# Constant matmuls in TensorE's waits, and the first attention's head choice as four masked output weights, in a four-layer network on one core

## The chip, the core and the metric

The kernel runs on one core of a Trainium2 chip. A core has engines that each work through an instruction list of their own in order: TensorE (PE; its weight loads are shown apart as PEld), VectorE (DVE), ScalarE (ACT), GpSimd (POOL) and SyncE (SP), the last issuing most DMAs. They meet through semaphores: an instruction raises one, another engine waits until it has reached a number. PSUM has eight banks of 128 x 512 float32 into which TensorE writes and from which DVE and ACT read. The metric is device time of the whole program in microseconds (us), less is better.

## The reference, cut to what matters

The input is x of shape (4, 512, 128), 2048 tokens of 128 features. Four layers follow each other, each an attention-like part and a feed-forward part; each part's result is added to x and the sum goes through a layer norm without weights. The parts differ from layer to layer: attention inside windows of 32 tokens with 16 heads of 8 features, then 16 experts (4 of them per token) and a shared one; attention by directions with 8 heads, then 8 experts of limited capacity; rotary attention with 8 heads of 128, then a block of rotary attention with 16 heads of 64 and 31 experts; a gated linear recurrence with a small feed-forward, then 8 experts. Only the first attention's arithmetic is arranged anew by the change:

```python
qkv = jnp.einsum('bglc,cd->bgld', xg, w_qkv)
q, k, v = jnp.split(qkv, 3, axis=-1)
q = rmsnorm(q, ln_w); k = rmsnorm(k, ln_w)
# 16 heads of 8 features, windows of 32 tokens
att = jnp.einsum('bghqd,bghkd->bghqk', q, k) * scale
att = softmax(where(causal, att, -max))
y = jnp.einsum('bghqk,bghkd->bghqd', att, v)
y = y.transpose(0, 1, 3, 2, 4).reshape(Bx, Tx, Cx)
return jnp.einsum('btc,cd->btd', y, w_proj)
```

## The kernel before, in words

x lies in SBUF feature-major, 128 features on the partitions and 2048 tokens along the rows, worked on in B = 4 blocks (chunks) of T = 512 columns. The program is a row of stages, in this order, with the names that the profile shows: load; window attention (`l0a`); norm with the router's logits, router and experts of layer 0 (`f_n0a`, `r`, `e`); norm and scores, then the direction attention (`a1p`, `a1`); norm, capacity router, capacity experts (indirect DMAs carry tokens to the experts' slots in DRAM and back); norm and rotary attention with whole heads (`a2f_n1f`, `a`); norm and rotary attention with two heads per unit (`h`), router, experts; norm and recurrence (`rc`); norm, router with a hidden layer, experts; a last norm with the store (`n3f`). Between stages `recycle` (L115) clears the semaphores and puts a barrier over all engines. Most stages begin with a `Head` (L259): TensorE centres each block (`centre`, L218 to 221: a matmul of the sum with `center_w`), ACT squares, TensorE takes the mean of squares (`variance`, L237 to 241), ACT makes the inverse root, DVE scales. A wait on `PEq L119` in the trace is this barrier's.

Inside a stage the order of every engine is written out by hand, as a list of calls with the semaphore waits between them. Nothing plans or reorders it; what an engine does next is what stands next in its list. So TensorE idles where its next instruction's inputs are not there.

Window attention (L405 to 664) takes one chunk at a time: chunk 0, a loop over chunks 1 and 2, then chunk 3. Per chunk TensorE does the scores (`scores`, L492 to 504, 64 small products of 32 rows), the previous chunk's output product (`out`, L509 to 511), the next chunk's projections (`front`, L478 to 490), and the values (`values`, L513 to 526). Each group of 32 partitions in the four PSUM banks of the values holds four heads side by side although a partition's feature belongs to only one of them. DVE picks the right head: with masks in `vecs` columns 1 to 4 it forms `y_fm` as a sum of four masked slices (L642, three times L644), and `out` multiplies that with `wproj`.

A float32 matmul of the program appears in the trace as two records: the centre product of one block is `x2`.

The routers (L1017) compute logits, wait for DVE to find the best experts, and then transpose the gates on TensorE (L1096). Experts (L718) run `hidden` (L855 to 857: products of rounded parts) ahead of `output` (L871 to 874). In the capacity experts (L1387) POOL issues 32 indirect DMAs (L1417), SP waits for all of them and loads the slots (L1429), TensorE turns them (L1444).

## Time and profile before

| | |
|---|---|
| median of 3 runs | 1823.33 us (1818.88 to 1825.23) |
| the profiled execution, its own time | 1824.96 us |
| its span | 1823.2 us |
| TensorE busy | 1552.0 us (85%) |
| VectorE busy | 1033.2 us (57%) |
| ScalarE busy | 1005.3 us (55%) |
| GpSimd busy | 758.9 us (42%) |
| mean granted TensorE clock | 0.918 |

The profiled execution is one run of the program; its span is from the first to the last instruction. Busy time is the time in which an engine executes, summed; TensorE's includes matmuls at whichever clock was granted. The granted clock is 1.0 at 2.4 GHz and 0.5 at 1.2 GHz. In a row of the timeline `[8.74 <-DVE r_g_tm L1187]` says that the engine had been idle for 8.74 us and that the instruction which released it was DVE's, on tile r_g_tm, in line 1187.

### The profile page before, as it was taken

What the parts mean: (1) busy time and instruction counts of PE and PEld (TensorE: products, weight loads), DVE (VectorE), ACT (ScalarE), POOL (GpSimd) and SP (SyncE); (2) the same over time, 40 slices, a digit from 0 to 9 for tenths busy, and PEclk for the clock granted to TensorE, in tenths of its full rate; (3) what the DMA queues carried; (4) which work ended last, traced back from release to release, by engine and by line L of the source; (5) the groups of instructions that cost most, each with busy time, mean ns of one, the idle gap of its engine ahead of it and who ended that gap; (6) DMA issues with size and microseconds to landing.
All of it is one profiled execution on the core that took longest, in us unless ns stands there. A gap on an engine that the chain in (4) does not pass through costs nothing. (4 is left out here: it accounts for less than half of the span.)

```text
span 1823.2 us, 27092 instructions
## 1 busy us (share of the span) xinstructions
PE 1552.0 (85%) x8756; PEld 999.4 (55%) x8756; DVE 1033.2 (57%) x2134; ACT 1005.3 (55%) x2164; POOL 758.9 (42%) x704
## 2 busy tenths in 40 slices
PE   5668987860977799999789999999889999858898
PEld 3336743330974566666445555555458886324685
DVE  5955776631214555555356556556458886662675
ACT  4324564550423455555556666656538887664786
POOL 1224530017342566666165655655324442021363
PEclk8968978975888999999999999999979999979899
DMA  1007311021223122222121111111026562000330
GB/s 42 1 15 166 75 61 52 1 96 47 78 65 114 40 60 62 60 59 59 62 55 42 42 48 43 40 47 44 15 89 262 211 217 89 1 0 21 136 113 24
DMA packets 62165, 125.50 MB, mean 69 GB/s; under 512 B 14354, under 2 KB 29571, under 8 KB 55532
## 3 DMA queue, kind: packets, MB, share of 16 engines
q1 hardware_dynamic: 59724, 119.57, 22.5%
q0 software_dynamic: 2304, 4.24, 0.7%
q8 instruction: 69, 1.13, 0.3%
q14 instruction: 68, 0.56, 0.1%
HBM read 79.39 MB, written 11.35 MB: 50 GB/s over the span
## 5 line engine op out<-in xcount | busy, mean ns | idle before, releaser
L1857 ACT ACTIVATE h_probs<-psum,h_nmax 128x512 f32<-128x512 f32 (+3 forms) x256 | 133.3, 526 | 126.0 <-DVE h_nmax L1937 68.2
L1937 DVE TENSOR_REDUCE h_nmax<-psum 128x1 f32<-128x512 f32 (+3 forms) x256 | 116.3, 486 | 101.5 <-PE psum L1747 101.5
L897 ACT ACTIVATE psum<-psum,f_b 128x512 f32<-128x512 f32 x200 | 131.8, 659 | 27.4 <-PE psum L857 27.3
L1672 POOL TENSOR_TENSOR h_swapped<-h_swapped,rope_tables 128x512 f32<-128x512 f32 x64 | 81.8, 1278 | 153.8 <-DMA h_swapped<-h_raw 153.8
L823 POOL TENSOR_TENSOR e_lo<-e_gated,e_hi 128x512 fp32r<-128x512 f32 x59 | 76.1, 1291 | 152.1 <-ACT e_hi L909 152.1
L1857 ACT ACTIVATE a_probs<-psum,a_nmax 128x512 f32<-128x512 f32 (+3 forms) x128 | 67.6, 528 | 125.0 <-DVE a_nmax L1937 76.8
L1672 POOL TENSOR_TENSOR a_swapped<-a_swapped,a2f_a_tables 128x512 f32<-128x512 f32 x64 | 82.8, 1294 | 124.5 <-DMA a_swapped<-a_raw 124.4
L932 DVE TENSOR_TENSOR e_lo<-psum,e_hi 128x512 fp32r<-128x512 f32 x168 | 114.8, 683 | 26.5 <-ACT psum L897 26.5
L855 PE MATMUL psum<-f_x_hi,f_w_hi 128*128 128x512 f32 x272 | 109.2, 402 | 5.9 <-DVE e_gated L946 4.1
L1744 PE MATMUL psum<-h_k,h_q 64*128 64x384 f32 (+3 forms) x512 | 104.9, 486 | 7.5 <-POOL h_k L1677 5.0
L1754 PE MATMUL psum<-ident,h_probs 128*128 128x128 f32 x640 | 108.7, 277 | 0.6 <-ACT h_probs L1857 0.4
L856 PE MATMUL psum<-f_x_hi,f_w_lo 128*128 128x512 f32 x272 | 108.5, 399 | 0.0
L857 PE MATMUL psum<-f_x_lo,f_w_hi 128*128 128x512 f32 x272 | 108.3, 398 | 0.0
L1937 DVE TENSOR_REDUCE a_nmax<-psum 128x1 f32<-128x512 f32 (+3 forms) x128 | 62.5, 489 | 71.0 <-PE psum L1747 69.8
L1744 PE MATMUL psum<-a_k,a_q 128*128 128x512 f32 (+3 forms) x256 | 91.9, 442 | 6.2 <-DVE a_wvo L1929 6.2
L874 PE MATMUL psum<-e_lo,f_w_hi 128*128 128x512 f32 x236 | 92.7, 393 | 1.9 <-DVE e_lo L932 0.9
L871 PE MATMUL psum<-e_hi,f_w_hi 128*128 128x512 f32 x236 | 92.6, 392 | 0.0
L872 PE MATMUL psum<-e_hi,f_w_lo 128*128 128x512 f32 x236 | 92.4, 391 | 0.0
L1772 PE MATMUL psum<-h_p_t,h_v 128*64 128x256 f32 (+3 forms) x512 | 89.9, 451 | 0.0
L946 DVE TENSOR_TENSOR psum<-psum,e_gate 128x512 f32<-128x512 f32 x96 | 67.2, 700 | 32.9 <-ACT psum L897 28.6
L1754 PEld LDWEIGHTS psum<-ident,h_probs 128*128 128x128 f32 x640 | 71.6, 141 | 24.0 <-ACT h_probs L1857 19.9
L1772 PE MATMUL psum<-a_p_t,a_v 128*128 128x512 f32 (+3 forms) x256 | 82.4, 444 | 0.0
(471 smaller groups left out, 4024.0 us busy)
## 6 DMA issues: line engine op xcount, KB each, us to landing
e_gate<-gates SPq DMA_DIRECT2D x39, 1024.0 KB, 4.7
a_swapped<-a_raw SPq DMA_DIRECT2D x128, 128.0 KB, 2.3
h_swapped<-h_raw SPq DMA_DIRECT2D x256, 64.0 KB, 2.0
e_gate<-gates SPq DMA_DIRECT2D x16, 512.0 KB, 7.2
f_w<-in_l_experts SPq DMA_DIRECT2D x17, 256.0 KB, 5.0
f_w<-in_l_experts SPq DMA_DIRECT2D x32, 128.0 KB, 4.7
slots<-a_empty SPq DMA_DIRECT2D x1, 2600.0 KB, 7.5
e_got<-slots SPq DMA_DIRECT2D x8, 325.0 KB, 5.6
```

The costliest lines, as they stand in the source:

```text
L855: nc.tensor.matmul(to, w_h, ex.x_hi[:, cols(b)], start=True, stop=False, skip_group_check=True)
L856: nc.tensor.matmul(to, w_l, ex.x_hi[:, cols(b)], start=False, stop=False, skip_group_check=True)
L857: nc.tensor.matmul(to, w_h, ex.x_lo[:, cols(b)], start=False, stop=True, skip_group_check=True).then_inc(hid_ready, 1)
L874: nc.tensor.matmul(to, w_h, lo[:, n % PLACES, :], start=False, stop=True, skip_group_check=True).then_inc(out_done, 1)
L897: nc.scalar.activation(to, hidden_bank(n), ex.act_func, **bias(n)).then_inc(act_ready, 1)
L932: nc.vector.tensor_tensor(lo[:, n % PLACES, :], whole, hi[:, n % PLACES, :].bitcast(F32), ALU.subtract).then_inc(lo_dve, 1)
L1672: nc.gpsimd.tensor_tensor(swapped[:, j, :], swapped[:, j, :], tables[:, 2 * j + 1, :], ALU.mult).then_inc(sin_ready, 1)
L1744: nc.tensor.matmul(ring[j % RING][:, 0:(q + 1) * P], qs[rows, U % 3, q * P:(q + 1) * P], ks[rows, U % 3, 0:(q + 1) * P], start=True, stop= ...
L1754: last = nc.tensor.transpose(ring[j % RING][:, k * P:(k + 1) * P], probs[:, j % 4, k * P:(k + 1) * P], core.ident[:])
L1772: last = nc.tensor.matmul(misc[1][d, k * P:T], stationary, p_t[:, U % 2, h, k, k * P:T], start=k == 0, stop=k == QT - 1, skip_group_check= ...
L1857: nc.scalar.activation(probs[:, j % 4, 0:(q + 1) * P], ring[j % RING][:, 0:(q + 1) * P], ACT.Exp, bias=nmax[:, j % 8:j % 8 + 1], accum_out ...
L1937: nc.vector.tensor_reduce(nmax[:, j % 8:j % 8 + 1], ring[j % RING][:, 0:(q + 1) * P], AX.X, ALU.max, negate=True).then_inc(max_ready, 1)
```

## The change

There is a new helper. It issues `n` float32 matmuls of two tables that stand in SBUF since the load, `mean_w` (128 x 128) and 256 columns of `rope_tables`, into a PSUM bank that nobody reads before it is written again. Its results are used nowhere. It is called at 45 places of TensorE's order (the seven heads of the direction attention's lead count one each), 225 matmuls in all: at the ends of stages (3 each), behind the stages' heads, and ahead of waits for other engines.

```diff
+def keep_busy(core, pe, bank, n):
+
+    for _ in range(n):
+        core.nc.tensor.matmul(core.psum[:, bank, 0:T // 2], core.mean_w[:], core.rope_tables[:, 0, 0:T // 2], start=True, stop=True)
...
     def tensor(self, pe):
         first, second = self.first, self.second
+        if not first.center:
+            keep_busy(self.core, pe, 7, 3)
```

In the window attention the choice of the head moves from DVE into the weights: four copies of `wproj`, each masked to the features of one head of its group, are made once by DVE, and `out` accumulates four products over head slices. The values are copied out of PSUM as they are, by ACT (in the last chunk half by ACT, half by DVE).

```diff
                 def out(c):
-                    pe.wait_ge(y_ready, c + 1)
-                    nc.tensor.matmul(ps_o[0], wproj[:], y_fm[:].rearrange("p w t q -> p t w q"), start=True, stop=True).then_inc(out_ready, 1)
+                    pe.wait_ge(y_ready, W * c + W)
+                    of_head = o_sb[:].rearrange("p w (t h q) -> p h t w q", h=HG, q=L)
+                    for h in range(HG):
+                        last = nc.tensor.matmul(ps_o[0], wproj_of[:, h, :], of_head[:, h, :, :, :], start=h == 0, stop=h == HG - 1)
+                    last.then_inc(out_ready, 1)
...
                     if not last:
                         front(c + 1)
+                    else:
+                        keep_busy(core, pe, 7, 12)
                     values(c, first, last)
+                    if last:
+                        keep_busy(core, pe, 0, 3)
...
-                pe.wait_ge(mask_ready, 1)
+                pe.wait_ge(mask_ready, 1 + HG)
                 front(0)
                 per_chunk(pe, chunk)
                 out(B - 1)
+                keep_busy(core, pe, 0, 2)
...
+                    act.wait_ge(av_ready, c + 1)
+                    if not first:
+                        act.wait_ge(out_ready, c)
+                    for w in range(2 if last else W):
+                        nc.scalar.activation(o_sb[:, w, :], ps_o[w], ACT.Copy).then_inc(y_ready, 1)
...
-                    dve.wait_ge(av_ready, c + 1)
-                    o = core.psum[:, 4:8, :].rearrange("p w (t h q) -> p (w t) h q", h=HG, q=L)
-                    to = y_fm[:].rearrange("p w t q -> p (w t) q")
-                    for h in range(HG):
-                        if h == 0:
-                            step(nc.vector.tensor_scalar(to, o[:, :, h, :], vecs[:, 1:2], None, ALU.mult))
-                        else:
-                            mix = nc.vector.scalar_tensor_tensor(to, o[:, :, h, :], vecs[:, 1 + h:2 + h], to, ALU.mult, ALU.add)
...
+                    if last:
+                        dve.wait_ge(av_ready, c + 1)
+                        dve.wait_ge(out_ready, c)
+                        for w in range(2, W):
+                            nc.vector.tensor_copy(o_sb[:, w, :], ps_o[w]).then_inc(y_ready, 1)
...
+                for h in range(HG):
+                    nc.vector.tensor_scalar(wproj_of[:, h, :], wproj[:], vecs[:, 1 + h:2 + h], None, ALU.mult).then_inc(mask_ready, 1)
```

The other calls of the helper, the important ones in the order of the program:

```diff
@@ experts: before the first hidden, and at the end @@
+                if not ex.gate_output:
+                    keep_busy(core, pe, 0, 4)
...
+                keep_busy(core, pe, 0, 3)
@@ router: before the wait for the gates @@
+                keep_busy(core, pe, 3, 20 if kind == "sigmoid_groups" else 7 if hidden else 0)
                 pe.wait_ge(gates_ready, 1)
@@ capacity router: before its wait @@
+                keep_busy(core, pe, 3, 10)
                 pe.wait_ge(chosen_ready, 1)
@@ capacity experts: 28 of the 32 indirect DMAs raise sent_first, the last four raise sent @@
+                pe.wait_ge(sent_first, 2 * (NT - 2) * 16)
+                keep_busy(core, pe, 0, 14)
                 turn(0)
...
                 output(E - 1, 1)
+                keep_busy(core, pe, 0, 16)
@@ scores of the directions: at the end, 9 behind a wait for the third block from the end @@
+                pe.wait_ge(rest_ready, len(items) - 3)
+                keep_busy(core, pe, 0, 9)
@@ direction attention: 3 first, 2 behind each of seven heads of the lead, 4 and 3 around second(0) @@
                     first_products(f, m_read)
+                    keep_busy(core, pe, 3, 2)
...
+                keep_busy(core, pe, 3, 4)
                 second(0)
+                keep_busy(core, pe, 6, 3)
@@ rotary attentions: 5 behind the head, 10 (whole heads) or 4 before the first scores @@
                 head.tensor(pe)
+                keep_busy(core, pe, 6, 5)
...
+                pe.wait_ge(raw_ready[1], AHEAD)
+                keep_busy(core, pe, 6, 10 if merged else 4)
                 scores(0)
@@ in the first unit, behind slots 3, 4, 5 and 7 @@
+                    if U == 0 and slot in (3, 4, 5, 7):
+                        keep_busy(core, pe, 7, 2)
@@ recurrence @@
                 z_gate(0)
+                keep_busy(core, pe, 4, 7)
...
                 gates(3)
+                keep_busy(core, pe, 2, 18)
                 out(0)
```

How this stands in the engines' lists. First TensorE at the end of the window attention, chunk 3 and the first products of the norm behind it; before:

```order
L504 MATMUL psum<-l0a_kx,l0a_qn 32x128 x64
L511 MATMUL psum<-l0a_y_fm,l0a_wproj 128x512
L526 MATMUL psum<-l0a_p_t,l0a_v_tm 32x128 x64
L511 MATMUL psum<-l0a_y_fm,l0a_wproj 128x512
L454 UNCONDITIONAL_BRANCH
L1065 UNCONDITIONAL_BRANCH
L221 MATMUL psum<-sum_fm,center_w 128x512 x2
```

and now:

```order
L513 MATMUL psum<-l0a_kx,l0a_qn 32x128 x64
L522 MATMUL psum<-l0a_o_sb,l0a_wproj_of 128x512 x4
L126 MATMUL psum<-rope_tables,mean_w 128x256 x12
L538 MATMUL psum<-l0a_p_t,l0a_v_tm 32x128 x64
L126 MATMUL psum<-rope_tables,mean_w 128x256 x3
L522 MATMUL psum<-l0a_o_sb,l0a_wproj_of 128x512 x4
L126 MATMUL psum<-rope_tables,mean_w 128x256 x2
L463 UNCONDITIONAL_BRANCH
L1085 UNCONDITIONAL_BRANCH
L227 MATMUL psum<-sum_fm,center_w 128x512 x2
```

The names: `l0a_kx`, `l0a_qn` are keys and queries of the scores, `l0a_p_t` the probabilities, `l0a_v_tm` the values, `l0a_o_sb` the copied values. Each output product became four, twelve constant matmuls stand ahead of the last values, three behind them and two at the end.

DVE at the end of a middle chunk and the beginning of the next one's softmax; before:

```order
L70 REGISTER_ALU
L601 TENSOR_SCALAR l0a_kx<-l0a_kn,l0a_vecs 128x16x32 x4
L642 TENSOR_SCALAR l0a_y_fm<-psum,l0a_vecs 128x512
L70 REGISTER_ALU
L644 SCALAR_TENSOR_TENSOR l0a_y_fm<-psum,l0a_vecs,l0a_y_fm 128x512
L70 REGISTER_ALU
L644 SCALAR_TENSOR_TENSOR l0a_y_fm<-psum,l0a_vecs,l0a_y_fm 128x512
L70 REGISTER_ALU
L644 SCALAR_TENSOR_TENSOR l0a_y_fm<-psum,l0a_vecs,l0a_y_fm 128x512
L450 REGISTER_ALU
L450 COMPARE_AND_BRANCH
L620 TENSOR_REDUCE l0a_smax<-psum 128x16
```

and now:

```order
L70 REGISTER_ALU
L623 TENSOR_SCALAR l0a_kx<-l0a_kn,l0a_vecs 128x16x32 x4
L459 REGISTER_ALU
L459 COMPARE_AND_BRANCH
L642 TENSOR_REDUCE l0a_smax<-psum 128x16
```

The four operations on `l0a_y_fm` are gone, so the first maximum (`l0a_smax`) stands directly behind the keys' masks.

TensorE around the first router's end; before:

```order
L1013 MATMUL psum<-f_rw,x_fm 128x16 x16
L714 MATMUL psum<-x_fm,ident 128x512 x4
L1096 MATMUL psum<-ident,r_g_tm 32x128 x16
L1054 UNCONDITIONAL_BRANCH
L838 UNCONDITIONAL_BRANCH
L855 MATMUL psum<-f_x_hi,f_w_hi 128x512
```

and now:

```order
L1033 MATMUL psum<-f_rw,x_fm 128x16 x16
L731 MATMUL psum<-x_fm,ident 128x512 x4
L126 MATMUL psum<-rope_tables,mean_w 128x256 x20
L1117 MATMUL psum<-ident,r_g_tm 32x128 x16
L1074 UNCONDITIONAL_BRANCH
L855 UNCONDITIONAL_BRANCH
L126 MATMUL psum<-rope_tables,mean_w 128x256 x4
L872 MATMUL psum<-f_x_hi,f_w_hi 128x512
```

Twenty constant matmuls stand between the transposes of x (`x_fm`) and the transposes of the gates (`r_g_tm`), and four ahead of the experts' first product.

## Rows read from the trace of the kernel before

**Rows 1.** The page: the span, and the granted clock in 40 slices, in tenths.

```profile
span 1823.2 us, 27092 instructions
...
PEclk8968978975888999999999999999979999979899
```

**Rows 2.** Windows (us, busy us by engine): sum over the 31 half-clock stretches.

```profile
sum 299.02, PE 169.10 PEld 102.00 DVE 121.07 ACT 79.08 POOL 94.48; mean PE 5.45 PEld 3.29 DVE 3.91 ACT 2.55 POOL 3.05
```

**Rows 3.** Windows: sum over the half-clock stretches at seven norm starts.

```profile
sum 37.56, PE 30.69 PEld 12.00 DVE 3.83 ACT 14.17 POOL 5.14; mean PE 4.38 PEld 1.71 DVE 0.55 ACT 2.02 POOL 0.73
```

**Rows 4.** Timeline (start, duration, engine, line): two norm starts.

```profile
108.64 3.75 PE L221 MATMUL psum<-sum_fm,center_w 128*128 128x512 f32 x4 [1.72 <-PEq L119]
...
113.90 1.32 PE L221 MATMUL psum<-sum_fm,center_w 128*128 128x512 f32 x2
...
555.22 1.95 PE L221 MATMUL psum<-sum_fm,center_w 128*128 128x512 f32 x4 [2.04 <-PEq L119]
...
558.09 1.02 PE L221 MATMUL psum<-sum_fm,center_w 128*128 128x512 f32 x2
...
558.95 1.02 PE L241 MATMUL psum<-a2f_n1f_sq,mean_w 128*128 128x512 f32 x2
```

**Rows 5.** Timeline: a middle chunk of the window attention.

```profile
59.21 3.41 PE L526 MATMUL psum<-l0a_p_t,l0a_v_tm 32*32 32x128 f32 x128 [1.36 <-ACT l0a_lnm L559]
...
64.68 0.74 DVE L642 TENSOR_SCALAR l0a_y_fm<-psum,l0a_vecs 128x512 f32<-128x512 f32 x1
...
64.90 1.89 PE L504 MATMUL psum<-l0a_kx,l0a_qn 32*32 32x128 f32 x128 [1.32 <-DVE l0a_kx L601]
65.45 2.32 DVE L644 SCALAR_TENSOR_TENSOR l0a_y_fm<-psum,l0a_vecs,l0a_y_fm 128x512 f32<-128x512 f32 x3
67.69 0.68 DVE L620 TENSOR_REDUCE l0a_smax<-psum 128x16 f32<-128x512 f32 x1
```

**Rows 6.** Timeline: the last chunk of the window attention.

```profile
96.40 5.24 PE L526 MATMUL psum<-l0a_p_t,l0a_v_tm 32*32 32x128 f32 x128 [7.60 <-DVE l0a_p_t L608]
...
96.91 1.96 DVE L608 STREAM_TRANSPOSE l0a_p_t<-l0a_p_sb 128x512 f32<-128x512 f32 x3
...
104.85 2.07 PE L511 MATMUL psum<-l0a_y_fm,l0a_wproj 128*128 128x512 f32 x2 [3.21 <-DVE l0a_y_fm L644]
```

**Rows 7.** Timeline: TensorE at a router and experts; windows: sum over four half-clock stretches there.

```profile
138.22 3.60 PE L1096 MATMUL psum<-ident,r_g_tm 128*32 128x128 f32 x16 [8.74 <-DVE r_g_tm L1187]
...
149.79 0.79 PE L855 MATMUL psum<-f_x_hi,f_w_hi 128*128 128x512 f32 x1 [4.08 <-DVE e_gated L946]
...
1359.18 0.79 PE L855 MATMUL psum<-f_x_hi,f_w_hi 128*128 128x512 f32 x1
...
sum 37.54, PE 23.02 PEld 15.59 DVE 19.51 ACT 9.05 POOL 3.61; mean PE 5.75 PEld 3.90 DVE 4.88 ACT 2.26 POOL 0.90
```

**Rows 8.** Timeline: first product of the capacity experts, and a window behind it.

```profile
453.08 0.97 POOL L1417 DMA_INDIRECT slots<-f_rows,f_slots  x1 [0.30 <-issue]
...
458.30 1.33 PE L1444 MATMUL psum<-ident,e_got 128*128 128x128 f32 x5 [51.38 <-DMA e_got<-slots]
...
458.30:466.07 7.77, 6.93 (x27) 6.56 (x28) 1.75 (x4) 3.37 (x9) 0.00 (x0) 0.50 0.74 267
```

**Rows 9.** Windows: sum over seven half-clock stretches at the other attentions' starts.

```profile
sum 61.46, PE 44.30 PEld 26.66 DVE 28.67 ACT 14.76 POOL 19.70; mean PE 6.33 PEld 3.81 DVE 4.10 ACT 2.11 POOL 2.81
```

**Rows 10.** Timeline: the third attention's first scores.

```profile
581.54 2.05 PE L1744 MATMUL psum<-a_k,a_q 128*128 128x512 f32 x2 [6.20 <-DVE a_wvo L1929]
```

**Rows 11.** Timeline: two waits of TensorE in the recurrence.

```profile
1562.99 3.75 PE L2609 MATMUL psum<-h_xn,h_w_in 128*128 128x512 f32 x4 [4.35 <-DVE rc_xc L2783]
...
1625.98 4.05 PE L241 MATMUL psum<-rc_g_sq,mean_w 128*128 128x512 f32 x4 [12.58 <-POOL rc_g_sq L235]
```

**Rows 12.** Timeline: the end of the first experts.

```profile
225.78 0.69 DVE L975 COPY sum_fm<-psum 128x512 f32<-128x512 f32 x1 [0.22 <-PE psum L874]
...
227.61 3.41 PE L221 MATMUL psum<-sum_fm,center_w 128*128 128x512 f32 x4 [1.86 <-PEq L119]
```

More of the change, by code:

```diff
@@ L1399, in capacity_experts @@
         hid = st.sb("hid", [P, 2, HT, CAPACITY])
-        (w1_split, sent, turned, x_rounded, x_split, hid_psum, hid_ready, out_psum, out_ready, returned, joined) = (st.sem(n) for n in (
-            "w1_split", "sent", "turned", "x_rounded", "x_split", "hid_psum", "hid_ready", "out_psum", "out_ready", "returned", "joined"))
+        (w1_split, sent_first, sent, turned, x_rounded, x_split, hid_psum, hid_ready, out_psum, out_ready, returned, joined) = (st.sem(n) for n in (
+            "w1_split", "sent_first", "sent", "turned", "x_rounded", "x_split", "hid_psum", "hid_ready", "out_psum", "out_ready", "returned", "joined"))
         got_loaded = [st.sem(f"got{e}_loaded") for e in range(E)]
@@ L1417, in _ @@
                         nc.gpsimd.indirect_dma_start(dram["slots"], bass.IndirectOffsetOnAxis(slots[:, k, t:t + 1], 0), rows[:, t, k, :], None,
-                                                     bounds_check=E * CAPACITY - 1, oob_is_err=False).then_inc(sent, 16)
+                                                     bounds_check=E * CAPACITY - 1, oob_is_err=False).then_inc(sent_first if t < NT - 2 else sent, 16)
                 for e in range(E):
@@ L1426, in _ @@
             def _(sp):
-                sp.wait_ge(sent, 2 * NT * 16)
+                sp.wait_ge(sent_first, 2 * (NT - 2) * 16)
+                sp.wait_ge(sent, 2 * 2 * 16)
                 for e in range(E):
@@ L1494, in _ @@
                     last.then_inc(joined, 1)
+                keep_busy(core, pe, 4, 3)
             @block.scalar
@@ L1835, in _ @@
                     between(NU, slot)
+                keep_busy(core, pe, 0, 3)
             @block.scalar
@@ L2344, in _ @@
                         m_read = top_ready, edge_done(f)
+                keep_busy(core, pe, 2, 3)
                 spread_sums(n_units - 1, m_read)
+                keep_busy(core, pe, 2, 5)
                 out(B - 1, (ln_ready, n_units))
+                keep_busy(core, pe, 2, 3)
             @block.scalar
@@ L2679, in _ @@
                     shrink(b)
+                keep_busy(core, pe, 5, 3)
             @block.scalar
```

10 lines of the change are left out of this document (4 added, 6 removed).

## The prediction

> **What bounds the kernel now.** I read the granted clock first. It falls to about 0.5 at stage starts and stays near 1.0 in the long middles [rows 1]; a view of windows over the 31 stretches at 0.5, that is 1.2 GHz, adds up to 299.0 us, in which TensorE is busy for 169.1 us [rows 2]. Work at 1.2 GHz takes twice its time at 2.4 GHz: four records of the centre product take 3.75 us at the half clock and 1.95 us at the full one [rows 4]. So if every stretch were at full clock, TensorE would do its 169.1 us in 84.6 us: 84.5 us is the most that the clock can give, less wherever DVE, ACT, POOL or a DMA sets the pace. What the clock has in common before each fall is a TensorE that waits: 8.74 us at the first router, 7.60 us before the last values, 51.38 us before the capacity experts [rows 6 to 8]. Then I read, stage by stage, which wait ends last.
>
> The Trainium skill, page "TensorE: Matmul & The Clock Gate", section "Terms", prices throttled time at the whole stretch times (1 - K/N), here 299.0 x 0.5 = 149.5 us by an estimate. The trace disagrees: only 169.1 us of the stretches holds TensorE work [rows 2].
>
> **Price of the constant products.** One float32 product of 512 columns follows the next 0.86 us later at full clock (558.09 to 558.95) [rows 4]; half as many columns is 0.43 us, and 0.86 us at the half clock. 225 of them are 97 us at full clock, 194 at half. They cost nothing while they end before the wait they stand in; else the rest is paid. Bounds on what they bring: all 84.5 us, or nothing (a gain below nothing is excluded only where the wait outlasts them at 0.86 us).
>
> **Window attention.** In a middle chunk the scores end at 64.90 + 1.89 = 66.79, but DVE's first maximum starts at 67.69 since it stands behind the y operations (65.45 + 2.32 = 67.77) [rows 5]. Without them it starts some 0.2 us behind the scores, 0.7 us earlier; at three chunk borders 2.1 us. The four ACT copies can run from the values' end (59.21 + 3.41 = 62.62) and are wanted at the scores' end, 4.2 us later: hidden, if ACT is free. The four output products take 3.4 us instead of 0.9 and delay the next projections, whose banks the softmax frees anyway in about 2 us: I take 0; the bound is +1.5 us a border. Four masks of the weights lie before the first product: no row shows 128 x 128; a 128 x 512 of this operation takes 0.74 us [rows 5], so 0 to 3.0 us; I take 0.2 each, 0.8. Last chunk: twelve products (5.2 us) stand in the 7.60 us wait. At full clock the values end when the last transposed group (96.91 + 1.96 = 98.87) has gone through TensorE, about 99.8, instead of 101.64: -1.8. Before, values to output end is 104.85 + 2.07 - 101.64 = 5.3 us [rows 6]; now two copies of about 0.65 in each of two engines, a semaphore, and 3.4 us: 5.1; -0.2. Sum -2.1 + 0.8 - 1.8 - 0.2 = **-3.3**.
>
> **Norm starts.** Seven norms begin at half clock, with 30.69 us of TensorE work [rows 3], so at most 15.3. From the first centre product to the third it is 5.26 us at half (108.64 to 113.90) against 2.87 at full clock (555.22 to 558.09) [rows 4]: 2.4 us at the two coldest, 1.2 to 1.6 at four others, 0.9 at the last: -11.4. The price is the three products at each of nine stage ends: 1.3 us, beside the copy that ends the stage, 0.69 us, and its semaphore [rows 12]. The barrier waits for TensorE too: about 0.45 us each, **+4.0**. Net **-7.4**.
>
> **Routers and experts.** Four stretches hold 23.02 us of TensorE work [rows 7], at most 11.5. First router: 20 x 0.43 = 8.6 us in a wait of 8.74, then the transposes at half of 3.60: -1.8. First experts: 5.7 us of work at half follow 149.79: -2.8. Last router: 7 products (3.0 us) fill less than half of a similar wait: -1.3 of 3.5. Experts of layer 2: the product at 1359.18 is behind no wait [rows 7], four products there are four times 0.43: +1.7, and that they turn the clock is not to be read from a row where TensorE was busy without a pause; 0. Capacity experts: SP still waits for the last indirect DMA, issued at 453.08; 14 products begin about 450.2 (the last four DMAs are issued 0.97 + 0.30 us apart, and the one before them must land) and take 6.0 us; TensorE's first turn was at 458.30. The 6.93 us behind it go at most to 3.5 [rows 8]: -3.0. Capacity router: -0.3. Sum -1.8 - 2.8 - 1.3 + 1.7 - 3.0 - 0.3 = **-7.5**.
>
> **Attentions.** Seven stretches hold 44.30 us of TensorE work [rows 9], at most 22.2, but 28.67 us of DVE lies beside it. In the direction attention DVE paces the lead, so a fraction: -2.5 us for the lead and the first steps (two products per head, 0.86 us, fit a head of 1.9 us only at full clock). Rotary with whole heads: ten products (4.3 us) in the 6.20 us wait [rows 10]: -3.0. With two heads per unit: -2.5. Sum **-8.0**, bounds 0 and -22.
>
> **Recurrence and router of layer 2.** The waits are 4.35 us (seven products, 3.0 us) and 12.58 us (18 products, 7.7 us, before two output products). Behind them 3.75 and 4.05 us at half clock become about 1.95 and 2.1 [rows 11]: -3.7. The rotary norm's first variance: -1.0. Sum **-4.7**.
>
> **Sum.** -3.3 - 7.4 - 7.5 - 8.0 - 4.7 = -30.9. Each term supposes that the clock stays up through its wait. As many waits keep an unfilled rest of 2 to 5 us, I take 0.87 of it: -27. Against the profiled execution's own 1824.96 us (span 1823.2) that is 1798; the runs' median, 1823.33, is 1.6 lower: **1796 us**. No DMA is added or moved past another: POOL still issues the 32 indirect ones in one run, and SP's wait, now on two semaphores, ends with the same last one.
>
> **Rivals.**
> 1. *The clock holds nearly everywhere.* Then half of all half-clock work on a path set by TensorE comes back. For: the stretches are few and short; filling one wait also spares what follows. Against: DVE and POOL are busy 121 and 94 us in the same stretches [rows 2]. Of 84.5 us, I leave out what is beside DVE in the attentions (10), the unfilled stretches (14) and the paid products (10), some 50 remain; less inevitable waits 45: 1824.96 - 45 - 1.6 = 1778.
> 2. *The clock is hardly held.* The products stand too thin in waits of which only a part is filled. Then only the window attention (-2) and a third of the clock's terms come, and the ends still cost 4: some -10, 1813.
> 3. *Slower: the products run at half clock and outlast their waits.* A product is then 0.86 us. The first router's 20 take 17.2 us against 8.74 [rows 7]: +8.5 us; the lead's 14 add 12.0; the capacity experts' 14 take 12.0 against about 8: +4; layer 2's four +3.4; nine ends 2.6 against 0.7: +17. Together 45, of which half is paid if the clock rises midway through each group, as it does before under steady work; less 3 from the window attention: +20, 1843. It decides from the point where groups end later than their wait. Against it: in the cold norm start the clock rises within the work itself, between the first product at 3.75 us for four records and the third at 1.32 for two, where full clock has 1.02 [rows 4].
> 4. *The page's rule.* That a half-clock stretch is paid whole: 1824.96 - 149.5 - 1.6 = 1674 us. As a mechanism of this kernel, other engines' waits would have to shrink with TensorE's clock; in the stretches TensorE is idle for 299.0 - 169.1 = 130 us [rows 2]. It is the rule of the Trainium skill named above.
>
> **How the numbers follow.** Forecast 0.58, rival 1 0.17, rival 2 0.15, rival 3 0.09, rival 4 0.01. The forecast's own range is 1783 to 1809. The range for 8 in 10 goes from 1776 to 1817: it takes in rival 1's middle and most of rival 2, and leaves out rivals 3 and 4 and the tails of 1 and 2. About 0.3% (5.5 us) is what a measurement can tell from no change. Within it lies a third of rival 2 and a little of rival 3 (0.07 in all); slower is most of rival 3: 0.08; faster 0.85.
>
> **What would show it.** Right: the granted clock of the 31 stretches falls from 299 us to under 150; the transposes behind the first router take 1.9 us instead of 3.6; the window attention's last values take about 3.4 us; third minus first centre product is 2.9 us at most norms; the products record 0.43 us each. Wrong: constant products of 0.86 us with the next real product behind them without a wait (rival 3); half-clock sums above 250 us (rival 2); stage ends that cost more than half a microsecond each; or the clock at 1.0 and DVE, ACT or POOL as releasers of every first product, with the same time as before.

## The result, and the profile after

The changed kernel takes 1802.28 us (median of 4 runs, 1797.98 to 1804.23), the kernel before 1824.28 us in the same comparison (median of 4, 1818.88 to 1829.33): a ratio of 0.9873, with a 95% interval of 0.9849 to 0.9896. That is 22 us less, where 27 to 28 were forecast. The profiled execution took 1802.68 us, its span is 1800.9 us.

The page of the changed kernel, the lines that answer to [rows 1], and TensorE's busy time, which was 1552.0 us before:

```profile
span 1800.9 us, 28045 instructions
...
PE 1621.8 (90%) x9230; PEld 1065.9 (59%) x9230; DVE 1018.5 (57%) x2124; ACT 1011.3 (56%) x2178; POOL 756.8 (42%) x704
...
PEclk8999999985998999999999999999979999989999
```

TensorE is busy 70 us longer and the program is 22 us shorter. The granted clock shows why. The windows over the 14 stretches that are left at half clock (us, then busy us by engine, the granted clock in the column before the last two), three of them and their sum, against [rows 2]:

```profile
394.43:442.21 47.78, 4.48 (x11) 3.05 (x11) 8.87 (x25) 0.00 (x0) 31.63 (x32) 0.50 0.13 42
...
568.50:578.75 10.25, 8.81 (x23) 5.68 (x24) 2.88 (x7) 2.65 (x7) 1.74 (x3) 0.50 0.17 38
...
1339.92:1346.74 6.82, 6.82 (x16) 4.78 (x15) 0.19 (x1) 0.66 (x1) 0.00 (x0) 0.50 0.72 236
...
sum 136.70, PE 83.02 PEld 52.48 DVE 49.51 ACT 30.52 POOL 58.15; mean PE 5.93 PEld 3.75 DVE 3.54 ACT 2.18 POOL 4.15
```

31 stretches with 299.0 us became 14 with 136.7 us; the TensorE work in them went from 169.1 to 83.0 us. Of these 83.0 us 11.4 are constant products (the same windows for L126 alone), so the program's own work at half clock fell from 169.1 to about 72 us. Half of that difference, some 48 us, is the most that the clock gave; 22 arrived.

Cut at the first centre product of each norm, the spans of the two traces compare as follows (us, from starts like those in [rows 4]; "again" is a second trace of each, see the experiments):

| stretch that ends at the next norm's start | before | again | after | again | difference of the first two |
|---|---|---|---|---|---|
| load, window attention | 108.64 | 108.45 | 104.32 | 104.44 | -4.3 |
| norm, first router, experts | 118.97 | 118.45 | 114.13 | 114.06 | -4.8 |
| norm, directions | 156.27 | 156.22 | 156.37 | 157.04 | +0.1 |
| norm, capacity router and experts | 171.35 | 168.78 | 167.21 | 164.50 | -4.1 |
| norm, rotary attention | 333.32 | 332.45 | 329.04 | 331.01 | -4.3 |
| norm, two-heads attention, router, 31 experts | 650.92 | 652.11 | 653.49 | 654.55 | +2.6 |
| norm, recurrence | 125.23 | 124.15 | 121.08 | 120.91 | -4.2 |
| norm, last router, experts | 141.93 | 141.27 | 140.21 | 140.24 | -1.7 |
| last norm, store | 16.54 | 16.26 | 15.00 | 15.00 | -1.5 |

**Norms.** The timeline of TensorE at the recurrence's norm, the stage end's products first (start, duration, engine, line):

```profile
1521.38 1.46 PE L126 MATMUL psum<-rope_tables,mean_w 128*128 128x256 f32 x6
1524.57 1.96 PE L227 MATMUL psum<-sum_fm,center_w 128*128 128x512 f32 x4 [1.73 <-PEq L119]
...
1527.43 1.02 PE L227 MATMUL psum<-sum_fm,center_w 128*128 128x512 f32 x2
```

The third centre product now starts 2.86 us behind the first; before it was 5.24 to 5.26 us at the three coldest norms [rows 4]. Over the eight norms this distance adds up to 35.9 us before and 24.8 us after: -11.0. A second trace of the kernel before has 32.3 us, since two more of its norms, the last two, start at full clock unaided (2.87 us); a second trace of the changed kernel has 24.8 again. One norm stays at 4.75 us in the changed kernel, the one before the directions. Its clock is 1.00 too, but a product that waits for a DMA stands ahead of the third centre product:

```profile
222.14 1.13 PE L2511 MATMUL psum<-a1w_spread,a1w_w 24*128 24x256 f32 x4 [0.66 <-DMA a1w_scale<-in_l_scale]
```

**Stage ends.** The end of the first experts, as [rows 12]:

```profile
215.86 1.46 PE L126 MATMUL psum<-rope_tables,mean_w 128*128 128x256 f32 x6
216.06 0.69 DVE L995 COPY sum_fm<-psum 128x512 f32<-128x512 f32 x1 [0.21 <-PE psum L891]
...
218.45 1.95 PE L227 MATMUL psum<-sum_fm,center_w 128*128 128x512 f32 x4 [1.13 <-PEq L119]
```

Six records are three products. From the end of the last real product (215.53 + 0.50 = 216.03) to the norm's first it is 2.42 us, where it was 1.86. At six of the stages' barriers it is +0.56, +0.54, +0.58, +0.55, +0.53 and +0.44: 3.2 us paid. Behind the window attention it is +0.1, at the last experts nothing.

**Window attention**, last chunk, as [rows 6]:

```profile
95.01 2.38 PE L538 MATMUL psum<-l0a_p_t,l0a_v_tm 32*32 32x128 f32 x96 [0.23 <-DVE l0a_p_t L630]
...
97.45 1.08 ACT L602 ACTIVATE l0a_o_sb<-psum 128x512 f32<-128x512 f32 x2 [7.06 <-PE psum L538]
...
98.79 3.70 PE L522 MATMUL psum<-l0a_o_sb,l0a_wproj_of 128*128 128x512 f32 x8
...
102.53 0.69 DVE L634 TENSOR_TENSOR sum_fm<-psum,x_fm 128x512 f32<-128x512 f32 x1 [3.79 <-PE psum L522]
```

The values end at 97.4 at full clock, the copies of ACT and DVE run side by side, and the four output products (eight records) take 3.70 us.

**First router and experts**, as [rows 7]. Eight records are the four products ahead of the experts:

```profile
134.07 1.97 PE L126 MATMUL psum<-rope_tables,mean_w 128*128 128x256 f32 x8 [0.93 <-PEq L1074]
135.69 0.58 PE L872 MATMUL psum<-f_x_hi,f_w_hi 128*128 128x512 f32 x1
...
141.10 0.50 PE L872 MATMUL psum<-f_x_hi,f_w_hi 128*128 128x512 f32 x1 [2.30 <-DVE e_gated L966]
```

The experts' first product is at full clock, and where 4.08 us of wait preceded half-clock work it is now 2.30 us, followed by 3.4 us at half clock.

**Capacity experts**, as [rows 8], with the last indirect DMA:

```profile
442.12 0.97 POOL L1439 DMA_INDIRECT slots<-f_rows,f_slots  x1 [0.30 <-issue]
...
447.38 0.77 PE L1467 MATMUL psum<-ident,e_got 128*128 128x128 f32 x5 [0.34 <-DMA e_got<-slots]
```

From the last indirect DMA's issue to the first turn it is 5.26 us, before 5.22: the turn is as late as its DMA allows. But its five records take 0.77 us instead of 1.33.

**Two places that are paid for.** The two-heads attention's first scores: four products (eight records) stand behind ACT's copy and run at half clock.

```profile
898.00 3.78 PE L126 MATMUL psum<-rope_tables,mean_w 128*128 128x256 f32 x8 [2.78 <-ACT h_raw L1880]
898.89 1.26 POOL L1704 TENSOR_TENSOR h_k<-h_rot,h_swapped 128x512 f32<-128x512 f32 x1
...
901.70 1.76 PE L1771 MATMUL psum<-h_k,h_q 64*128 64x512 f32 x4
```

POOL has `h_k` ready at 898.89 + 1.26 = 900.15, but the scores start at 901.70, behind the products. And the experts of layer 2, where there is no wait at all:

```profile
1336.77 4.06 PE L860 MATMUL psum<-f_gates_t,f_b 32*128 32x512 f32 x8 [0.93 <-PEq L1074]
1340.76 3.78 PE L126 MATMUL psum<-rope_tables,mean_w 128*128 128x256 f32 x8
1343.98 0.99 PE L872 MATMUL psum<-f_x_hi,f_w_hi 128*128 128x512 f32 x1
```

The products take 3.2 us (1340.76 to 1343.98), 0.8 each, inside a stretch at half clock that is there as before, 1339.92 to 1346.74.

**Two places where the wait only moved.** The rotary attention, against [rows 10], and the recurrence, against [rows 11]:

```profile
560.47 4.58 PE L126 MATMUL psum<-rope_tables,mean_w 128*128 128x256 f32 x20 [0.63 <-ACT a_raw L1880]
...
568.98 2.05 PE L1771 MATMUL psum<-a_k,a_q 128*128 128x512 f32 x2 [3.92 <-DVE a_wvo L1962]
```

```profile
1591.25 7.93 PE L126 MATMUL psum<-rope_tables,mean_w 128*128 128x256 f32 x36
1599.02 3.60 PE L2675 MATMUL psum<-rc_h,h_w_out 128*128 128x512 f32 x8
1607.42 4.05 PE L247 MATMUL psum<-rc_g_sq,mean_w 128*128 128x512 f32 x4 [4.80 <-POOL rc_g_sq L241]
```

The first scores of the rotary attention wait 3.92 us behind ten products (twenty records) and stand in a stretch at half clock all the same (568.50). In the recurrence 18 products fill 7.9 us, and 4.80 us of wait for POOL remain: what comes next is set by POOL and DVE.

### The profile page after: what moved, and what is told of

Its sections match the earlier page's. It is cut to its first block and busy times, and to the rows that moved or that the text cites. A ratio compares the mean times of both kernels' runs of the same rounds, so it can differ in the third digit from the quotient of the medians.

```text
span 1800.9 us, 28045 instructions
## 1 busy us (share of the span) xinstructions
PE 1621.8 (90%) x9230; PEld 1065.9 (59%) x9230; DVE 1018.5 (57%) x2124; ACT 1011.3 (56%) x2178; POOL 756.8 (42%) x704
## 5 line engine op out<-in xcount | busy, mean ns | idle before, releaser
L1970 DVE TENSOR_REDUCE h_nmax<-psum 128x1 f32<-128x512 f32 (+3 forms) x256 | 116.1, 485 | 103.9 <-PE psum L1774 103.9
L126 PE MATMUL psum<-rope_tables,mean_w 128*128 128x256 f32 x450 | 111.7, 397 | 50.0 <-DMA slots<-f_rows,f_slots 43.3
L1699 POOL TENSOR_TENSOR h_swapped<-h_swapped,rope_tables 128x512 f32<-128x512 f32 x64 | 81.7, 1276 | 156.3 <-DMA h_swapped<-h_raw 156.3
L126 PEld LDWEIGHTS psum<-rope_tables,mean_w 128*128 128x128 f32 x450 | 86.7, 198 | 70.9 <-DMA slots<-f_rows,f_slots 44.0
```

Source lines behind the costliest of these rows:

```text
L126: core.nc.tensor.matmul(core.psum[:, bank, 0:T // 2], core.mean_w[:], core.rope_tables[:, 0, 0:T // 2], start=True, stop=True)
L1699: nc.gpsimd.tensor_tensor(swapped[:, j, :], swapped[:, j, :], tables[:, 2 * j + 1, :], ALU.mult).then_inc(sin_ready, 1)
L1970: nc.vector.tensor_reduce(nmax[:, j % 8:j % 8 + 1], ring[j % RING][:, 0:(q + 1) * P], AX.X, ALU.max, negate=True).then_inc(max_ready, 1)
```

## The experiments

All were run in groups that share the runs of the kernel before; ratios are to it. A granted clock c over a span s means 2 x (1 - c) x s at half clock. What a trace of an experiment shows inside a stage is given as time from the first centre product of that stage's norm.

**The head choice alone.** The helper issues nothing:

```diff
-    for _ in range(n):
+    for _ in range(0):
```

> The changed kernel with no constant product issued anywhere; the head choice in four masked weights stays. Theory (the two parts are independent, and the head choice is worth what DVE's y operations held on the path): the window attention ends some 2 to 3 us earlier (no clock gain in its last values), everything behind it as before; 1821 us, ratio to before 0.998 to 0.999. Rival (the products carry nothing, the whole gain of 22 us is from the head choice or from where the code lies): 1802. Half-clock time in the 31 stretches: near 299 us by the theory, near 139 by the rival.

1816.46 us (12 runs), ratio 0.9979, interval 0.9954 to 1.0005. Span and mean granted clock:

```profile
core 0: 1814.9 us, clock 0.920
```

0.16 x 1814.9 = 290 us at half clock, as before. The window attention's stretch is 104.2 us against 108.6 and 108.5: -4.3 us, more than expected, and as much as in the changed kernel. The last values end at 97.41 us without any constant product, at 97.39 in the changed kernel, and the norm behind the stage starts at full clock (2.87 us) in both. The gain in the whole is within what the interval allows: it is not told from none.

**The products alone.** The window attention of the kernel before with its own 17 products, all else as changed.

> The 225 constant products as in the changed kernel, the window attention otherwise as before (y formed by DVE, one output product). Theory: 18 to 20 us of the 22 come from the products: 1805, half-clock time near 140 us, norms from first to third centre product 2.9 us. Rival (the four output products in the last chunk are needed to keep the clock for the first norm): the first norm starts at half clock again (third minus first centre product 5.3 us) and 3 us more are lost: 1808.

1801.21 us (6 runs), ratio 0.9893 (0.9868 to 0.9919): all of the gain, as far as can be told. The window attention's stretch is 105.7 us, -2.9 us. So its two halves don't seem to add: each alone brings 3 to 4 us there and both together 4.3, though seven traces of kernels that differ from the changed one at most in the two products at this stage's end have 103.9 to 105.6 us. The first norm's distance is 2.87 us, so the rival, that the norm needs the four output products, is out: the products alone or, in the trace before this one, the output products alone are enough.

**The same places, hardly any work.**

```diff
-        core.nc.tensor.matmul(core.psum[:, bank, 0:T // 2], core.mean_w[:], core.rope_tables[:, 0, 0:T // 2], start=True, stop=True)
+        core.nc.tensor.matmul(core.psum[:, bank, 0:4], core.mean_w[:], core.rope_tables[:, 0, 0:4], start=True, stop=True)
```

> All 225 constant products at their places, but 4 columns wide instead of 256, so that TensorE's order, waits and semaphores are those of the changed kernel and only the work of the products is gone. Theory (what helps is that TensorE is at work in the waits, and so keeps its clock): the half-clock time goes back to 280 to 300 us and the time to about 1819 us (the head choice's 3 to 4 us remain, 4 us for the wider products at stage ends are saved, 4 come from less at the experts of layer 2 and the two-heads attention). Rival (the order, the earlier weight loads or the changed wait on the indirect DMAs bring the gain): 1800, with the half-clock time high all the same. Rival 2 (any activity is enough for the clock): half-clock time stays near 139 us and the time falls below the changed kernel's, about 1792.

1826.93 us (12 runs), ratio 1.0029 (1.0009 to 1.0049): slower than before. The products' line and the clock:

```profile
L126 PE MATMUL psum<-rope_tables,mean_w 128*128 128x4 f32 x450 | 69.9, 282 | 52.6 <-DMA slots<-f_rows,f_slots 43.3 <-PEq L2111 3.0 <-ACT h_raw L1880 2.8
```

```profile
core 0: 1821.5 us, clock 0.921
```

0.158 x 1821.5 = 288 us at half clock. Order, waits and semaphores are those of the changed kernel, so the gain is the clock's and not the order's; both rivals are out. With nothing but their width taken away some 25 to 28 us are lost against the full products (by the medians and by the ratios); against the head choice alone, measured beside it, the kernel is 0.5% slower, about 9 us: the instructions by themselves cost that.

**No products at stage ends.** 26 products gone.

> The changed kernel without the products at the ends of the stages (2 at the window attention's, 3 at the last output of experts, direction attention, rotary attentions, recurrence, capacity experts). Theory of the prediction: each of nine ends costs 0.45 us (in the changed trace about 0.6), and the seven norm starts behind them are at full clock only because of them: the cost of 4 to 5 us goes and 6 to 11 us of norm starts come back, time 1804 to 1808. Rival (the clock would have held over the barrier without them, since what stands before is steady work): norms stay at 2.9 us from first to third centre product and the time falls by 4 to 5 us to about 1797.

1799.55 us (6 runs), ratio 0.9884 (0.9858 to 0.9911), not told apart from the changed kernel. The barriers are back at 1.86 to 2.56 us, so 3.2 us are saved; three of the norm starts fall to half clock again (4.35, 5.25 and 4.23 us from first to third centre product), the directions' is at 5.50 instead of 4.75, and the norm behind the window attention and three more stay at 2.87: 6.0 us lost in the sum over the norms. Both theories were half right: some starts hold their clock over the barrier unaided. The span is 4.7 us shorter in this one trace, mostly in stretches that also differ by 1 to 3 us between two traces of one kernel. Whether the products at stage ends are worth their price is not shown.

**Trim.** No products before the experts of layer 2, none in the first unit of the two-heads attention; there six ahead of the wait instead of four behind it:

```diff
-                if not ex.gate_output:
+                if name == "e0":
                     keep_busy(core, pe, 0, 4)
...
-                    if U == 0 and slot in (3, 4, 5, 7):
+                    if merged and U == 0 and slot in (3, 4, 5, 7):
...
-                pe.wait_ge(raw_ready[1], AHEAD)
-                keep_busy(core, pe, 6, 10 if merged else 4)
+                if merged:
+                    pe.wait_ge(raw_ready[1], AHEAD)
+                keep_busy(core, pe, 6 if merged else 0, 10 if merged else 6)
```

> The changed kernel with three groups taken out or moved: the four products before the experts' first product of layer 2 (the trace of the changed kernel shows no wait there and products at half clock), the eight products in the first unit of the two-heads attention, and its four before the first scores, which become six ahead of the wait instead of four behind it (another PSUM bank). Theory (these three are paid in full: 3.4, 2 to 3, and 1.5 us): the stage from the norm before the two-heads attention to the norm behind its experts, 653.5 us in the changed kernel, falls to 646 to 648, the whole to about 1796. Rival (they hold the clock for what follows, so without them the stretches at half clock grow there): the stage stays at 653 or goes to 656, the whole at 1802 or above.

1798.08 us (5 runs), ratio 0.9844 (0.9820 to 0.9869), whose interval overlaps the changed kernel's. The stretch with the two-heads attention and its experts takes 648.8 us, 4.7 less than in the changed kernel (653.5, again 654.6): 2.9 us of it between the gates' transposes and the experts' first product (7.14 against 10.05 us), 1.9 between the 1st and the 41st record of the scores, 0.5 before them. At the first scores:

```profile
896.32 2.76 PE L126 MATMUL psum<-rope_tables,mean_w 128*128 128x256 f32 x12
...
900.16 1.26 POOL L1704 TENSOR_TENSOR h_k<-h_rot,h_swapped 128x512 f32<-128x512 f32 x1
...
901.47 1.13 PE L1771 MATMUL psum<-h_k,h_q 64*128 64x512 f32 x4 [2.40 <-POOL h_k L1704]
```

Now TensorE waits for `h_k`, as before the change, and not `h_k` for TensorE. Three later kernels with the same trim have 648.0, 647.8 and 650.2 us there. The theory holds; the rival, that these products hold the clock for what follows, does not.

**Doubled at five waits.**

> The changed kernel with the products doubled at five waits, each in a stage of its own: first router 20 to 40, capacity experts 14 to 28, before the rotary attention's first scores 10 to 20, recurrence 18 to 36, last router 7 to 14. Theory (a product costs nothing until its wait ends, then 0.43 us at full clock): first stage with the router +7.7 (8.6 more, 0.9 of wait left), capacity experts +5.5, rotary attention +0.4 (3.9 us of wait left for 4.3) and some of its 10 us at half clock back, -3; recurrence +2.9 (4.8 of wait left for 7.7) less 2.8 for the work at half clock behind it; last router -1 to -2 (3.0 more in 4.4 left). Sum +12: 1814. Rival (half-clock products, 0.86 us each, wherever the wait outlasts the clock): the same sites +17, +12, +4.7, +10, 0; about 1840.

1814.96 us (6 runs), ratio 0.9927 (0.9901 to 0.9953); 1814 was expected. By the ratios it is some 10 us more than the changed kernel, where 12 were expected. The first router:

```profile
121.93 17.43 PE L126 MATMUL psum<-rope_tables,mean_w 128*128 128x256 f32 x80
139.19 1.91 PE L1117 MATMUL psum<-ident,r_g_tm 128*32 128x128 f32 x16
```

Eighty records take 17.43 us, so one product 0.436 us at full clock; the gates' transposes start 35.27 us behind the norm's start, 8.4 us later than without any product (26.91): 40 x 0.436 - 8.76 = 8.7. Sum by stretch against the changed kernel: first router's +9.3, capacity experts' +7.4 (+10.1 against the changed kernel's second trace), recurrence +2.3, last router -0.5, rotary attention -4.6 (in one trace). The rival's 0.86 us per product is out, but for places like the two-heads attention's, where the clock has fallen before the products start.

**None at the same five waits**, 69 products fewer.

> The changed kernel with no products at the same five waits, all others kept. Theory of the prediction: back come 1.8 and 2.8 us in the stage of the first router, 3.0 at the capacity experts, 3.0 at the rotary attention, 1.9 at the recurrence, 1.3 at the last router: +14, 1816; half-clock time from 139 to about 200 us. Rival (the gain sits elsewhere, at the norms and stage ends): +4, 1806.

1806.66 us (6 runs), ratio 0.9889 (0.9864 to 0.9914); the 0.9873 of the changed kernel is not told from it, but the 1816 expected (0.9955) lies above its interval, so +14 us is out. At half clock are 0.092 x 1800.8 = 166 us, where about 200 were expected. TensorE around the first router and the second wait behind it:

```profile
132.55 3.52 PE L1117 MATMUL psum<-ident,r_g_tm 128*32 128x128 f32 x16 [8.76 <-DVE r_g_tm L1208]
...
145.50 0.50 PE L872 MATMUL psum<-f_x_hi,f_w_hi 128*128 128x512 f32 x1 [3.78 <-DVE e_gated L966]
```

The transposes are at half clock again (3.52 us) and the thirteenth record of the experts' first line comes at 49.78 instead of 46.71 us: by this pair the group brings 3.1 us. The record has less from other traces: with no product anywhere the same record comes at 48.36 us, and with the narrow ones, whose transposes are at half clock too, at 47.09, since there the clock is up again for the experts' products. So it is 0.4 to 3.1 us, by where the half-clock stretch falls. The others, against the changed kernel: capacity experts +0.5 (from the first turn of the slots to the join, the products that add the experts' rows up again, it is 84.2 against 82.3 us); recurrence -0.2; last router -1.0; rotary attention -3.9. The last router's products cost time: its stretch is 139.2 us in all four kernels without them and 140.2 to 140.8 in five traces with the seven. With them the experts' first product is at half clock (0.76 to 0.77 us), without them at full (0.47). Four of the five groups, which the prediction priced at 9.2 us together, bring little or nothing at their stage's end in this trace.

**Lean**: the trimmed kernel without those four groups.

> The trimmed kernel with four more groups taken out, those that the runs before showed to bring little or nothing: 14 ahead of the capacity experts, 10 before the rotary attention's first scores, 18 in the recurrence, 7 in the last router (the first router keeps its 20). Theory (the runs' marks inside the stages: recurrence 0.2, last router 1.0 and capacity experts' stage 0.5 us apart without them): as the trimmed kernel within 2 us, 1796 to 1799, with half-clock time 30 us higher. Rival (every group is worth what its half-clock work says, 0.5 of it): 5 to 8 us slower than the trimmed kernel, 1804.

1795.83 us (6 runs), ratio 0.9867 (0.9837 to 0.9896), half-clock time 0.086 x 1793.1 = 154 us. The span is as the theory has it (1793.1 against the trimmed 1795.5), and no stretch is over 2 us longer. By the ratios, which come from different comparisons and overlap, it is some 4 us slower than the trimmed kernel, so the times don't exclude the rival's 5 us.

**Lean, with eight products ahead of the first scores.**

```diff
                 def chunk(c, first, last):
+                    if first:
+                        keep_busy(core, pe, 7, 8)
                     scores(c)
```

> The lean kernel with eight products added ahead of the window attention's first scores, where TensorE waits 4.2 us in both kernels and 8.3 to 8.6 us of work at half clock follow. Theory (work behind a wait speeds up where TensorE sets the pace): the 10.2 us at half clock there go, the last chunk's values and so the stage end 1.5 to 3 us earlier (stage 104.2 to about 102). Rival (DVE and ACT set the pace of the first chunk, the projections at half clock end before they are wanted): the stage stays within 0.5 us.

1797.64 us (5 runs), ratio 0.9865 (0.9837 to 0.9893). From 16 to 42 us of the lean kernel, and of this one:

```profile
16.00:42.00 26.00, 17.53 (x164) 9.67 (x164) 14.07 (x29) 13.28 (x22) 5.05 (x7) 0.80 0.00 1
```

```profile
16.00:42.00 26.00, 19.50 (x259) 11.75 (x264) 15.34 (x31) 13.51 (x23) 6.32 (x8) 1.00 0.00 1
```

The clock holds (0.80 to 1.00) and the stretch is 102.7 instead of 104.1 us: -1.4, just short of the 1.5 expected and no match for the rival's 0.5; the last kernel below has 103.1 us with the same eight, against 103.9 to 105.6 without. In the whole it is not to be seen.

**Each kernel once more.**

> The kernel before once more, for the spread of its own trace. Theory (in two stages the changed kernel's difference is not the products' but chance: the direction attention's values, 93.0 us in the first trace, and the rotary attention's first 40 scores, 58.7 us): the stage of the directions, 156.3 us, comes out 2 to 8 us longer, or the rotary attention's, 333.3, 2 to 5 us shorter, the other stages within 0.5 us. Rival (both are properties of the kernel): all stages within 1 us.

> The changed kernel once more, for its spread. Theory: the stage of the directions within 2 us of 156.4 since the lead no longer falls to half clock, the rotary attention's stage anywhere from 324 to 330, all others within 0.7 us of the first trace. Rival: the rotary attention's stage at 329 again.

The table above has both. My theory fell for the directions: the kernel before gives 156.22 after 156.27, so nothing shows a chance in the trace of before; the changed kernel's 156.4 and 157.0 stand among 156.3 to 159.3 in kernels with the same code there. It is half right for the rotary attention: 332.5 and 331.0 in the second traces leave 1.4 us of a difference of 4.3, and the other kernels give 324.5 to 335.8, in no order of their products (the head choice alone, with none, 329.8). The capacity experts' stretch differs by 2.6 and 2.7 us between two traces of one kernel, the two-heads attention's by 1.2 and 1.1, the recurrence's by 1.1 in the kernel before: both the rival's 1 us for all stages and my 0.7 us for the changed kernel were too narrow. A difference of one stretch in one pair of traces is read with this in mind.

**Best of these**: lean, with the eight, and the capacity experts' 14 put back.

> The lean kernel with the eight products ahead of the first scores, and with the 14 ahead of the capacity experts put back, the one group of the four that showed a gain inside its stage (first turn to join 82.3 us with, 84.2 without). Theory: first turn to join 82.4 us again, the stage 1 to 2 us shorter than 165.6 to 168.1, the whole 1793 to 1797. Rival (the end of that stage is set by the tokens' way back through DRAM and not by TensorE): the join starts earlier but the stage is not shorter, the whole at 1796 to 1799 as without.

1794.44 us (6 runs), ratio 0.9839 (0.9812 to 0.9866): 31 us less than the kernel before here, and the lowest ratio of all, though its interval overlaps the changed kernel's. From first turn to join it is 82.6 us. Without the 14 it is 84.2, 82.3 and 83.1 in three kernels, with them 80.5 to 82.6 in six traces, so the two ranges touch, and the 1.9 us on which I put them back rest on one pair of traces; the stretch, 166.8 us, is inside its spread. That the 14 are worth their place is not shown.

## Why the prediction was right, and where it was not

Right were the side, the mechanism and the first bound: the clock is what is gained, and it comes only where TensorE sets the pace. The time, 1802.28, is 6 us above the forecast and inside its range. One sign that was named for being wrong did come: five stage ends cost more than half a microsecond each; all together they cost 3.3 us, where 4.0 were forecast. Term by term, forecast against measured in the traces:

| term | forecast | measured | from |
|---|---|---|---|
| window attention | -3.3 | -4.3 | its stretch; again -4.0 |
| norms, gained | -11.4 | -11.0 | first to third centre product |
| stage ends, paid | +4.0 | +3.3 | six barriers, and 0.1 |
| routers and experts | -7.5 | about -4.1 | below |
| attentions | -8.0 | about -3.1 | below |
| recurrence, router of layer 2 | -4.7 | about -2.9 | 2.8 us are gained before the gates, 2.3 given back to DVE and POOL by the second mean of squares, 2.2 stand at the stage's end |

*Window attention*: the -1.8 us that the prediction gave to its twelve constant products is not shown as theirs. The head choice alone, without any of them, brings the stage to 104.2 us and its last values to their end at the same time; only beside the old head choice do the constant products show a gain there, 2.9 us in one trace. From the last values' end to the last output product's it is 5.1 us, as forecast.

The norms are the part that the rows of before could price, since both clocks stood in them, and they came out within 0.4 us. Some of that is luck. Three norms were at 5.24 to 5.26 us and not two, which makes 12.9 us to gain and not 11.4; the directions' norm gave 0.5 of its 2.4 us, because of the product that waits for its DMA. Against the second trace of before the gain is 7.5 us, and the 2.4 us behind the window attention come with the head choice alone too.

*Routers and experts*: the first router with its experts gave 2.8 us (22.58 to 19.81 us from the transposes to the thirteenth record) and not 4.6: the step "5.7 us of work at half follow: -2.8" failed, since the second wait, 2.3 us still, has no product in it and half clock follows it again for 3.4 us. Layer 2's four products cost 2.5 us and not 1.7, the step "four times 0.43" failed: they stand in a half-clock stretch which I had in [rows 7] and left out of their price. The capacity experts' -3.0 was 3.2 us from the first turn to the join and about 2.9 at the end, the stage end's 0.58 counted apart; how much of it the 14 products bring is not shown. The last router's -1.3 failed: its stage is 1.7 us shorter, 1.2 of it in the norm, and without the seven products it is 1.0 us shorter still.

*Attentions*: this is the term that was mis-sized. In the directions the first values come 0.8 us earlier than before, 0.5 of it the norm's, and nothing is left at the end. That is against the kernel before; against the head choice alone, which takes 164.4 us there, the changed kernel is 8.0 us shorter, and these two differ by the products alone. In the two-heads attention it is 1.7 us worse and not 2.5 better: products that wait for ACT start at half clock and end behind `h_k`, and eight more in a unit without waits are paid. With layer 2's experts this is rival 3 in small: the mechanism that was given 0.09 for the whole was at work in two stages. The rotary attention shows -4.3 and -1.4 in two pairs, but the doubling and the removal of its ten products both left it shorter, and it takes 326.3 to 331.0 us in five traces with the ten and 325.2 to 330.3 in four kernels without them: the products' share of it is not shown.

*The factor 0.87* was too mild: -30.9 was added up, 22 came, a factor of 0.71. The clock was held as well as I thought (137 us were left at half clock, under the 150 named). But of the 48 us that it gave at most, some 7 to 8 went into paid products (3.3 at stage ends, 2.5 at layer 2's experts, 1.7 in the two-heads attention). The other 18 or so did not arrive, and more than that, since the head choice's part of the 22 us needs no clock; where traces show it, as in the recurrence, they went into waits for DVE and POOL, and they are not accounted for one by one. Rival 4, the whole stretch paid at half, which I named beside the Trainium skill's page "TensorE: Matmul & The Clock Gate", section "Terms", is out: 162 us fewer at half clock would have been 81 us by it, and 22 were measured.

That 20 products in 8.74 us of the first router are free was right to a tenth: the transposes start at 26.90 us with them and 26.91 without.

*The clock's falls.* The prediction read in the rows that TensorE waits before each of them. That does not hold for one before the experts of layer 2: from 1339.92 us the clock is at half, and TensorE was busy for 12.73 of the 13.66 us ahead of it.

What stays open: why the direction attention takes 164.4 us in the trace of the head choice alone, with a first stretch at half clock of 41.0 us, and 161.4 with the narrow products (30.7 us), against 156.3 with 27.3 in both traces of before, whose order there is the same but for one wait. With it stays open what the products bring in this stage.

## What to carry to other kernels

Idle time of TensorE ahead of work that it alone paces can be filled with constant products, here free up to the length of the wait (8.74 us at the first router); price the work behind at both clocks from rows, and count only that which no other engine ends. Look for the product that starts only when another engine has released it: at the two-heads attention it ran at half clock and stood in front of the real work when that became ready. And many such groups can bring nothing: here taking out 49 of the 225 in four waits, and 12 that were paid, gave a kernel with the ratio 0.9867 against 0.9873, no loss that could be measured. Which of the groups that are left carry the gain was not taken apart.

## What the runs showed that I had not expected

- The narrow products: 450 records of 128 x 4 have a mean of 282 ns against 397 ns for 128 x 256, so 225 products of almost no work still made the kernel about 9 us slower than none.
- The clock can be at half in the midst of unbroken work: from 1339.92 to 1346.74 TensorE is busy for 6.82 of 6.82 us, in both kernels at the same place of the program (before: 6.83 of 6.83 us from 1356.94), and from 1312.61 for 13.65 of 13.65 us.
- The first forty records of the rotary attention's scores take 49 to 59 us from kernel to kernel, with no change to them. Why is not shown.
